# Three of the four row tiles of the first attention's values are projected one batch ahead, inside the cross attention; their SBUF homes and those of the feed-forward weights move

## The reference

```
# layer 0: masked attention onto the context, 16 heads of 64
q = x @ W_Q.T + b_Q;  k = ctx @ W_K.T + b_K;  v = ctx @ W_V.T + b_V     # 512 x 1024 each
x = softmax_over_keys(q k^T / 8, masked) @ v @ W_O.T + b_O + x
# layer 1: gated mix with the mean over the rows of ctx, then a layer norm
# layer 2: causal attention onto ctx, 16 heads of 16, relu projections, norm
# layer 3: banded self attention, norm; full cross attention onto ctx, norm;
#          gelu(x @ w1 + b1) @ w2 + b2, norm
```

## Time and profile before

| | |
|---|---|
| Median of 3 runs | 1665.5 us (1665.3 to 1668.46) |
| Profiled execution | 1661.7 us, span 1659.9 us |
| TensorE busy | 1453.6 us (88%) |
| VectorE, ScalarE busy | 862.2 us (52%), 726.6 us (44%) |
| GpSimd busy | 262.9 us (16%) |
| Mean granted TensorE clock | 0.952 |

### The profile page before, as it was taken

How to read it: one execution, slowest core, us unless ns; L and a number is a source line. 1 busy time by engine, 2 the same in 40 slices (tenths; PEclk the granted TensorE clock), 3 DMA queues, 4 the chain that set the end, 5 groups by cost and what they waited for, 6 DMA issues and landing times.

```text
span 1659.9 us, 24194 instructions
## 1 busy us (share of the span) xinstructions
PE 1453.6 (88%) x8304; PEld 723.7 (44%) x8332; DVE 862.2 (52%) x2116; ACT 726.6 (44%) x1193; POOL 262.9 (16%) x129
## 2 busy tenths in 40 slices
PE   4999788788999889878999988887899998889786
PEld 2336445333533655432543464452253355455234
DVE  2672564482466355556156546455625635644651
ACT  0662354265166234427336425353724632625361
POOL 1004122201100313210110213221011030313001
PEclk9999799989999989989999998997999998999799
DMA  9001204503100220350310021223121004032300
GB/s 345 1 1 37 47 2 77 112 4 114 59 1 7 39 39 9 70 114 1 121 53 1 8 52 25 47 70 76 43 79 52 1 8 76 2 66 55 59 26 13
DMA packets 44087, 83.44 MB, mean 50 GB/s; under 512 B 10416, under 2 KB 27824, under 8 KB 43696
## 3 DMA queue, kind: packets, MB, share of 16 engines
q1 hardware_dynamic: 38912, 68.19, 16.1%
q10 hardware_dynamic: 5040, 13.54, 3.8%
HBM read 41.84 MB, written 2.10 MB: 26 GB/s over the span
## 4 chain that ended last, share of the span: by engine, by line
PE 67%; DVE 14%; issue 10%; ACT 5%; DMA 3%; ACTq 2%; POOL 0%; DVEq 0%; POOLq 0%
PE ring L1348 7%; PE ring L1183 7%; PE obank L1193 7%; PE ring L1134 7%; PE ring L1173 7%; DVE nmax L998 6%; PE obank L1398 4%; PE ring L1165 3%; PE ring L1249 3%; PE ring L1155 3%; PE obank L1114 3%; PE ring L1339 3%; PE ring L1121 3%; ACT q_all L728 2%; DMA q_all<-q_parts 2%
## 5 line engine op out<-in xcount | busy, mean ns | idle before, releaser
L998 DVE TENSOR_REDUCE nmax<-ring 128x2 f32<-128x1024 f32 (+1 forms) x192 | 219.2, 1176 | 72.1 <-PE ring L1348 56.4
L633 ACT ACTIVATE region_e<-region_d,nmin 128x512 f32<-128x512 f32 x256 | 182.6, 714 | 81.8 <-DVE nmin L851 80.2
L851 DVE CUSTOM_DVE_ANT_0 region_d<-ring,maskb 128x512 f32<-128x512 f32 x256 | 165.9, 687 | 93.7 <-issue 93.7
L741 ACT ACTIVATE region_e<-ring 128x1024 f32<-128x1024 f32 x192 | 183.3, 992 | 52.8 <-PE ring L1348 30.8
L728 ACT ACTIVATE q_all<-ring 2x1024 fp32r<-2x1024 bf16 x96 | 97.5, 1016 | 220.5 <-PE ring L1409 219.9
L558 POOL TENSOR_TENSOR nat_x<-nat_n,rows 128x1024 f32<-128x1024 f32 x16 | 37.6, 2348 | 630.9 <-DVE nat_n L896 461.2
L994 DVE TENSOR_REDUCE nmax<-ring 128x4 f32<-128x512 f32 (+1 forms) x96 | 87.3, 913 | 89.9 <-PE ring L1339 88.1
L1339 PE MATMUL ring<-cbf 64*128 64x128 bf16 (+2 forms) x1280 | 132.8, 287 | 0.0
L1183 PE MATMUL ring<-region_q 64*128 64x512 f32 x512 | 126.1, 613 | 5.4 <-ACT region_q L622 5.4
L1348 PE MATMUL ring<-k_tiles_a,q_all 64*128 64x512 f32 (+4 forms) x384 | 84.6, 485 | 45.3 <-DMA q_all<-q_parts 36.0
L1193 PE MATMUL obank<-region_e,vs 128*64 128x512 f32 x512 | 124.0, 605 | 0.0
(11 more groups left out here) (175 smaller groups left out, 2216.0 us busy)
## 6 DMA issues: line engine op xcount, KB each, us to landing
k_tiles_a<-k_parts SPq DMA_DIRECT2D x144, 64.0 KB, 2.3
k_tiles_b<-k_parts SPq DMA_DIRECT2D x144, 64.0 KB, 2.3
q_all<-q_parts ACTq DMA_DIRECT2D x144, 64.0 KB, 3.3
q_all<-q_parts SPq DMA_DIRECT2D x144, 64.0 KB, 2.8
region_b<-in_w_f SPq DMA_DIRECT2D x8, 1024.0 KB, 5.2
wvo<-in_wv SPq DMA_DIRECT2D x4, 1024.0 KB, 8.1
wqk<-in_wq SPq DMA_DIRECT2D x4, 1024.0 KB, 10.1
wqk<-in_wk SPq DMA_DIRECT2D x4, 1024.0 KB, 12.1
```

The costliest lines, as they stand in the source:

```text
L633: ins = act.activation(e0[:, n % E0, h, :], sm0[:, n % 2, h, :], ACT.Exp, bias=nmin0[:, n, h:h + 1], scale=-1.0, accum_out=sum0[:, n, h:h ...
L741: act.activation(e16[:, n % 4, 2 * u:2 * u + 2, 0:nq], slot((a, "B", g, kt, u))[:, :, 0:nq], ACT.Exp)\
L851: ins = dve.tensor_tensor_reduce(out=sm0[:, n % 2, h, :], in0=slot(("S0", p, kt))[:, h, :], in1=maskb[:, :], scale=-1.0, scalar=3.0e38, op ...
L998: dve.tensor_reduce(nmax[:, qt, 2 * u:2 * u + 2], slot(name)[:, :, 0:nk], AX.X, ALU.max, negate=True)\
```

## The change

`V0` tile 3 stays at the head of a batch. Tiles 0 and 1 of the next batch's values are projected behind `QC`, in the place of `keep_warm(6)`. Tile 2 is projected behind `OC`, and `turn(4)` keeps 2 of its 18 matmuls of `keep_warm`. DVE drains them there, and makes the next batch's mask and mean behind tile 2's drain. Ahead of the loop PE and DVE do the same three tiles, the mask and the mean for the first batch. In the last batch the three tiles are projected from the first batch's context, and nobody reads them. For this `wv0` is loaded again between the stacking for CAUSAL and that for BANDED, and `w_f1` and `w_f2` move to `region_e`, buffers 2 and 3 of the exponentials, so that `w_f1` is loaded at the end of FULL too. The tiles' homes in `region_b` are chosen so that 0 and 1 lie outside `k_tiles_a`.

```
 def plan_jobs():
-    jobs = [("V0", t) for t in range(NT)] + [("QK0", 0)]
+    jobs = [("V0", 3), ("QK0", 0)]
...
-    jobs += attention_jobs(BANDED) + [("KC",)] + [("OS", j) for j in range(2)] + [("X", 3), ("QC",)]
-    jobs += attention_jobs(FULL) + [("OC", j) for j in range(2)] + [("X", 4)]
+    jobs += attention_jobs(BANDED) + [("KC",)] + [("OS", j) for j in range(2)] + [("X", 3), ("QC",), ("V0", 0), ("V0", 1)]
+    jobs += attention_jobs(FULL) + [("OC", j) for j in range(2)] + [("V0", 2), ("X", 4)]
...
-        v0 = region_b[:, :].rearrange("p (t n) -> p t n", t=NT)
-        w_f1 = region_b[:, 2048:4096].rearrange("p (t n) -> p t n", t=DT)
-        w_f2 = region_b[:, 0:2048].rearrange("p (t n) -> p t n", t=FT)
+        v0 = [region_b[:, 1024 * t:1024 * (t + 1)] for t in (2, 3, 0, 1)]
+        w_f1 = region_e[:, 4096:6144].rearrange("p (t n) -> p t n", t=DT)
+        w_f2 = region_e[:, 6144:8192].rearrange("p (t n) -> p t n", t=FT)
...
 SP, batch b:
+                stack(CAUSAL, b)
+                for j in range(2):
+                    sp.wait_ge(*filled_by(("O0", j), b))
+                load(wv0, io["wv0"].rearrange("(t p) n -> p t n", p=P), "wv0")
+                stack(BANDED, b)
...
+                load_ctx((b + 1) % B)
+                stack(FULL, b)
+                sp.wait_ge(*filled_by((FULL, "B", GROUPS - 1, NT - 1, 1), b))
+                sp.wait_ge(pv_done, b * PV_ITER + UNITS0 + 3 * UNITS - 1)
                 load(w_f1, io["w_f1"].rearrange("(t p) n -> p t n", p=P), "ff")
+                sp.wait_ge(pv_done, b * PV_ITER + UNITS0 + 3 * UNITS)
                 load(w_f2, io["w_f2"].rearrange("(t p) n -> p t n", p=P), "ff")
                 if b + 1 < B:
-                    load(wv0, io["wv0"].rearrange("(t p) n -> p t n", p=P), "wv0")
                     load(wq0, ...)
                     load(wk0, ...)
...
 DVE:
+            for t in range(AHEAD):
+                drain_v0(t, (filled[t], 1), t)
+            mask_and_mean(0, first_link)
             with dve.Fori(0, B) as b:
+                drain_next(3)
...
                 drain_q(2, ("QC",), "cbq")
+                drain_next(0)
+                drain_next(1)
                 attention(FULL)
                 dve.wait_ge(resid_ready, b * 5 + 3)
                 drain_out("OC", nat_x)
                 norm(3)
+                drain_next(2)
+                mask_and_mean(b + 1, link)
...
 PE:
+            for t in range(AHEAD):
+                pe.wait_ge(drained[t], 1)
+                values_of_context(ring[:, t, :, :], t).then_inc(filled[t], 1)
             with pe.Fori(0, B) as b:
+                values0_of(3)
...
-                        keep_warm({1: 10, 2: 4, 3: 18, 4: 18}[n])
+                        keep_warm({1: 10, 2: 4, 3: 18, 4: 2}[n])
...
                 def attention(a):
-                    keep_warm(6)
+                    if a != FULL:
+                        keep_warm(6)
...
                 project_x(3, ("QC",), w_sq["cq"], range(DT))
+                pe.wait_ge(k_loaded["ctx"], b * 16 + 32)
+                pe.wait_ge(k_loaded["wv0"], b * 16 + 32)
+                values0_of(0)
+                values0_of(1)
                 attention(FULL)
                 out_heads(FULL, "OC")
+                values0_of(2)
                 turn(4, nat_n)
```

More of the change, by code:

```diff
@@ L159 @@
 ROUNDS = len(JOBS) // SLOTS
+AHEAD = 3
+FIRST_ROUNDS = AHEAD // SLOTS
+FIRST_LINKS = 6
 DVE_LINKS = 102
@@ L453, in _ @@
             for b in range(B):
-                for t in range(NT):
-                    sp.wait_ge(*filled_by(("V0", t), b))
+                sp.wait_ge(*filled_by(("V0", 3), b))
                 if b:
@@ L792, in _, with drain_v0, mask_and_mean, first_link @@
             dve.wait_ge(setup_act, 4)
+            def drain_v0(t, fill, at):
+                dve.wait_ge(*fill)
+                dve.tensor_tensor(v0[t], ring[:, at, :, :].rearrange("p a n -> p (a n)"),
+                                  row("bv0", 4).rearrange("p a n -> p (a n)"), ALU.add).then_inc(drained[at], 1)
+            def mask_and_mean(n, link):
+                dve.wait_ge(k_loaded["mask"], n * 16 + 16)
+                link(dve.tensor_scalar(maskb[:, :], mask_i, 0.0, NEG, ALU.is_equal, ALU.mult))
+                link(dve.tensor_reduce(nanfix[:, 0:1], maskb[:, :], AX.X, ALU.max))
+                link(dve.tensor_scalar(nanfix[:, 1:2], nanfix[:, 0:1], 0.0, None, ALU.is_equal))
+                link(dve.reciprocal(nanfix[:, 2:3], nanfix[:, 1:2]))
+                link(dve.tensor_scalar(nanfix[:, 3:4], nanfix[:, 2:3], 0.0, None, ALU.mult))
+                dve.wait_ge(k_loaded["ctx"], n * 16 + 16)
+                link(dve.tensor_reduce(small[:, 0:2], ctx_t[:, :, :], AX.X, ALU.add))
+                dve.tensor_scalar(pooled[:, :], small[:, 0:2], 1.0 / S, None, ALU.mult).then_inc(pooled_ready, 1)
+                dve.wait_ge(pooled_ready, n + 1)
+                dve.tensor_copy(spread[:, :, :], pooled[:, :].unsqueeze(2).broadcast_to([P, DT, P])).then_inc(spread_ready, 1)
+            first_links = [0]
+            def first_link(ins):
+                first_links[0] += 1
+                ins.then_inc(dve_link, 1)
+                dve.wait_ge(dve_link, first_links[0])
+            for t in range(AHEAD):
+                drain_v0(t, (filled[t], 1), t)
+            mask_and_mean(0, first_link)
+            assert first_links[0] == FIRST_LINKS, first_links
             with dve.Fori(0, B) as b:
@@ L800, in link @@
                     ins.then_inc(dve_link, 1)
-                    dve.wait_ge(dve_link, b * DVE_LINKS + links[0])
+                    dve.wait_ge(dve_link, FIRST_LINKS + b * DVE_LINKS + links[0])
                 holds = [0]
@@ L808, in hold, with drain_next @@
                     holds[0] += 1
[L811 to L828 removed]
+                def drain_next(t):
+                    drain_v0(t, filled_by(("V0", t), b), JOB["V0", t] % SLOTS)
+                drain_next(3)
+                dve.wait_ge(*drained_by(("V0", 3), b))
                 def scale_v(n):
@@ L1101, in _, with values_of_context @@
             pe.wait_ge(setup_pool, 6)
+            def values_of_context(dst, kt):
+                for i in range(2):
+                    for t in range(DT):
+                        ins = pe.matmul(dst[:, i, :], ctx_t[:, t, kt * P:(kt + 1) * P], wv0[:, t, i * 512:(i + 1) * 512],
+                                        start=(t == 0), stop=(t == DT - 1))
+                return ins
+            pe.wait_ge(k_loaded["ctx"], 16)
+            pe.wait_ge(k_loaded["wv0"], 16)
+            for t in range(AHEAD):
+                pe.wait_ge(drained[t], 1)
+                values_of_context(ring[:, t, :, :], t).then_inc(filled[t], 1)
             with pe.Fori(0, B) as b:
@@ L1156, in out_project, with values0_of @@
                         ins.then_inc(*ends_fill((name, j)))
-                pe.wait_ge(k_loaded["ctx"], b * 16 + 16)
-                pe.wait_ge(k_loaded["wv0"], b * 16 + 16)
-                for kt in range(NT):
-                    dst = start(("V0", kt))
-                    for i in range(2):
-                        for t in range(DT):
-                            ins = pe.matmul(dst[:, i, :], ctx_t[:, t, kt * P:(kt + 1) * P], wv0[:, t, i * 512:(i + 1) * 512],
-                                            start=(t == 0), stop=(t == DT - 1))
-                    ins.then_inc(*ends_fill(("V0", kt)))
+                def values0_of(t):
+                    values_of_context(start(("V0", t)), t).then_inc(*ends_fill(("V0", t)))
+                values0_of(3)
                 def qk(p):
```

44 lines of the change are left out of this document (12 added, 32 removed).

## The result

The changed kernel took 1639.1 us in the median of four runs, the kernel before 1665.4 us beside it. The ratio is 0.9834, with a 95% interval of 0.9811 to 0.9856. One of the four runs (1665.36 us) was disturbed; the ratios leave such runs out, and so do the medians from here on (1636.84 us for this set). A second set of five runs gave 1637.8 us and a ratio of 0.9845 (0.9823 to 0.9867). By the ratios the kernel is 26 to 28 us faster, where 32.7 us were forecast. The profiled execution took 1641.36 us, its span is 1639.5 us and its mean granted clock 0.953.

The account below looks back on a forecast made before the run. PE was taken as the bound, with `V0` whole on the chain at batch heads. Heads 28.8 plus clock 4.4 minus first batch 0.5 gave 32.7 us off 1665.5: 1633 us, range 1628 to 1643 us.

Parts of the forecast that it names:

- The head, 28.8 us: Heads of batches 2 to 4: three `V0` tiles less save 10.4 us each, less 0.8 us waiting for DVE's drain.
- The first rival: Batch heads: PE waits for ACT or DVE, ACT returning 4 us late, 4 us lost a head; 1643 us, one in ten.
- The first batch, -0.5 us: Start of the first batch: DVE does mask and mean before tile 3's drain and then enters the loop; 0.5 us lost.
- The two tiles in the cross attention hidden: Behind `QC`: tiles 0 and 1, 6.9 us, fit into PE's wait for DMAs, with 1.0 us to spare in the first batch.
- the test that I had set: Cross attention: the prediction is wrong if the scores start later behind `QC` than 11.4 us.
- The clock term, 4.4 us: Cross attention's start: without PE's idle time the clock stays 1.00 and the maxima end earlier; 4.4 us over four batches.
- the clock is not won back: Ahead of the cross attention a pause remains and the clock stays low; gain 28.3 us, 1637 us, one in ten.
- Tile 2, the weights: Behind `OC`, tile 2 replaces `keep_warm` at no cost, at most 0.2 us a batch; `w_f2` lands 3.7 us before `F1`.
- the rival that `F1` waits for its weights: At `F1`, late weights make PE wait; slower by over 0.2% at 9.0 us a batch, three in a hundred.

Follow-up runs that it names:

- markers: The changed kernel with one small instruction that waits for nothing at the loop's head on DVE and on ACT; 1640.49 us (one run).
- before_warm: The kernel before, with 31 instead of 6 `keep_warm` matmuls ahead of the cross attention; 1663.88 us against 1665.6, ratio 0.9991.
- before_again: The kernel before, unchanged, profiled a second time; 1666.43 us (one run).
- swap: The changed kernel with `QK0` ahead of `V0` tile 3 at the head of a batch; 1630.75 us, ratio 0.9801.
- cross_no_drain: The changed kernel with a one-element memset in place of each of DVE's drains of tiles 0 and 1 ahead of the cross attention; 1644.12 us (one run).

## Why the prediction was right, and where its size was off

The mechanism was right at the heads, for tile 2 and for the weights, and these make up the gain. The clock term was sized too high, and the DMAs ahead of the cross attention did not stay as they were. The time lies in the range of 1628 to 1643 us, but at or above the upper end of the 1629 to 1637 us that had seven chances in ten. The forecast of 1633 us was 4 to 6 us too low.

**The head, 28.8 us: right.** The stage with the heads fell by 28.3 us. DVE's jump cost 4.3 us rather than 3.98, and PE waited 0.91 us where 0.6 to 0.8 were expected. From `QK0` to Q2 the later batches take 139.0 us instead of 137.9, so a head loses 1.1 us rather than 0.8. The first rival, ACT coming back late, did not happen: markers measured its jump at 2.45 us, hidden under tile 3 and `QK0`. The prediction had weighed the Trainium skill here, "Runtime: NRT & Kernel Launch", section "Instruction fetch mechanics": a taken branch out of the fetched pages stalls the engine. The runs fit it for ACT as for DVE, at a little over half of DVE's price: two 8 KB packets of "q14 instruction" start at 439.3 and 439.9 us, within DVE's idle time from 436.97 to 441.31. PE shows no such gap at its own jump, although the prediction read the rule as one for every engine with a long body.

**The first batch, -0.5 us: not to be told from the spread.** Its stage took 0.2 us more, and two profiles of the kernel before differ by 1.2 us there.

**The two tiles in the cross attention hidden: right for PE, with 1.52 us to spare.** But the test that I had set, scores not later than 11.4 us behind `QC`, failed in three batches of four (12.09, 11.21, 12.02, 12.13). The prediction says that none of those DMAs depends on the new work. Their data don't, but their timing does: with PE's new code a load of instructions falls in among their issues, which took 8.3 to 9.0 us instead of 7.8.

**The clock term, 4.4 us: this is the term that was mis-sized.** The step says that the maxima, once back to back, end the cross attention earlier by what they save. They did run back to back: over four batches the eight maxima took 4.6 us less (means of two profiles each). But the forecast had the first one a little earlier behind `QC` than before, and it came 1.5 us later, as the sixth part landed late. So the maxima ended 3.1 us earlier and not 4.4. Behind them 1.0 us was lost to stretches of low clock, and 2.1 us are left: -4.8 us behind the first scores, +2.7 us ahead of them. In before_warm, with the clock effect alone, 4.1 us came and 3.7 went, and the time stayed. I had priced the maxima by themselves, and neither what stands ahead of them nor what follows. The rival "the clock is not won back", 1637 us, came nearest to the time, but by luck: the clock was won back at the place named.

**Two terms that were missing.** DVE's code moved, and its norm ahead of `QC` starts 0.35 us later in each batch: 1.4 us. BANDED took 5.6 us more in the mean, by stretches of low clock. This is the largest part of the miss. before_again shows that one program varies there by 3.5 us. That kernels with this head take more on average, and those with swap's head less (150.1 to 153.5 us), is seen in fourteen profiles and not explained.

**Tile 2, the weights: nothing, as predicted.** From `OC`'s end to `F1` no row waits for the weights, and the rival that `F1` waits for its weights fell.

**What stays open.** Why the sixth part lands 2.4 us after its issue in one batch, 3.5 in another and 4.4 in before_warm: DVE's drains aren't needed for it (cross_no_drain), nor the projection's matmuls (before_warm). What adds a stretch of low clock behind maxima that end early. And what lowers the clock in BANDED.

## What to carry to other kernels

Work that depends on nothing of its own iteration can go into an earlier wait, and the gain is its length on the path less what the restart now shows: look at which engine is idle without a releaser behind the jump, and put ahead what needs that engine least, as swap does. Price a wait's clock effect by the stages around it too, the one ahead of the place that gets faster and the one behind it, and test it alone before it is counted. Work that is hidden in a DMA wait still changes an engine's code: look where its loads of instructions then fall. Profile the kernel before twice: here its two spans differ by 4.7 us, as much as the forecast's error.

## What the runs showed of the hardware

- Behind the jump back to the loop's head the engines come back differently late: DVE 4.3 to 4.4 us, ACT 2.45 us idle without a wait. On PE none is seen: `V0` starts at 432.16, directly behind `F2`.
- When a 16 KB packet of the queue "q8 instruction" fell among the DMA issues of ACT and SP, both queues paused in the changed kernel's first batch for 1.3 to 1.5 us, and the DMA queues then moved next to nothing for about 0.6 us (21, 0 and 20 GB/s in slices of 0.2 us). ACT's twelve issues took 8.1 to 9.7 us in 38 such batches, and 7.6 to 7.8 us in the 18 others.
- One small instruction more on DVE took away a gap of 0.35 us that stood much later in its program, in each of four batches (13.15 instead of 13.51 us, in three kernels alike). An 8 KB packet of "q14 instruction" stands 0.6 to 0.9 us behind the gap wherever it is seen.
- Constant matmuls ahead of a stretch did not keep its clock: with 17 instead of 6 ahead of BANDED it still fell to 0.75.
